# Attention heads of a four-layer kernel: queries and keys as two 12-bit parts in fp32r words instead of three bf16 parts

## The reference, cut to what matters

```python
# layer 0, one sequence of 2048
scores = einsum('bhtd,bhsd->bhts', q, k) * scale       # scale = 8 ** -0.5
attn = softmax(scores, axis=-1)
out = einsum('bhts,bhsd->bhtd', attn, v)

# layer 3: q and k turned by rope, and causal
score = einsum('bhqd,bhkd->bhqk', rope(Q), rope(K)) / sqrt(8)
score = score - 1e10 * (1 - tril)
weights = softmax(score - max(score), axis=-1)
attn = einsum('bhqk,bhkd->bhqd', weights, V)
```

## Time and profile before

| what | value |
|---|---|
| time, median of 3 runs (lowest, highest) | 1925.89 us (1922.76, 1926.48) |
| span of the profiled execution, first to last instruction | 1923.2 us |
| own time of the profiled execution | not recorded apart from its span |
| PE matmul busy | 1697.7 us (88%) |
| DVE busy | 1435.9 us (75%) |
| ACT busy | 1143.8 us (59%) |
| POOL busy | 307.7 us (16%) |
| heads of layer 0 | from 47.3 to 744.9 us |
| heads of layer 3 | from 1396.4 to 1850 us |

### The profile page before, as it was taken

How to read it: one execution, slowest core, us unless ns; L and a number is a source line. 1 busy time by engine, 2 the same in 40 slices (tenths; PEclk the granted TensorE clock), 3 DMA queues, 4 the chain that set the end, 5 groups by cost and what they waited for, 6 DMA issues and landing times. The chain is left out here.

```text
span 1923.2 us, 44062 instructions
## 1 busy us (share of the span) xinstructions
PE 1697.7 (88%) x17529; PEld 802.7 (42%) x17529; DVE 1435.9 (75%) x2718; ACT 1143.8 (59%) x2262; POOL 307.7 (16%) x460
## 2 busy tenths in 40 slices
PE   3799999999999995889997798892779999999977
PEld 2222222222222222434444544781425555555556
DVE  5889999999999954665555507656779999999735
ACT  3268888888888894332222244452317777777754
POOL 0103000010000100000000345443012232210123
PEclk8789999999999998799997899996759999999988
DMA  4112111121111012033233269861511111111132
GB/s 143 36 30 81 63 55 51 55 81 64 55 51 34 28 28 59 33 66 106 95 89 144 69 225 333 268 186 48 191 33 30 33 37 37 34 36 36 28 76 70
DMA packets 78037, 154.52 MB, mean 80 GB/s; under 512 B 18684, under 2 KB 35964, under 8 KB 74136
## 3 DMA queue, kind: packets, MB, share of 16 engines
q1 hardware_dynamic: 63034, 121.38, 20.0%
q0 software_dynamic: 14384, 29.29, 4.9%
q10 hardware_dynamic: 414, 1.04, 0.2%
HBM read 102.23 MB, written 48.89 MB: 79 GB/s over the span
## 5 line engine op out<-in xcount | busy, mean ns | idle before, releaser
L856 ACT ACTIVATE heads_probs<-heads_pS 128x512 f32<-128x512 f32 (+3 forms) x1664 | 851.6, 573 | 187.9 <-PE heads_pS L725 172.2
L881 DVE TENSOR_REDUCE heads_run_max<-heads_pM 128x1 f32<-128x1024 f32 x512 | 592.6, 1216 | 54.6 <-PE heads_pM L747 53.3
L787 PE MATMUL heads_pO<-heads_probs,heads_vh 128*32 128x512 f32 (+2 forms) x3328 | 438.1, 570 | 3.2 <-ACT heads_probs L856 1.4
L725 PE MATMUL heads_pS<-heads_qs,heads_ks 75*32 75x512 bf16 (+3 forms) x4160 | 392.7, 370 | 3.8 <-ACT heads_probs L856 1.6
L892 DVE TENSOR_REDUCE heads_run_max<-heads_pM 128x1 f32<-128x512 f32 x384 | 246.7, 684 | 17.2 <-PE heads_pM L725 13.7
L725 PE MATMUL heads_pS<-heads_q_first,heads_ks 75*32 75x512 bf16 x2496 | 234.4, 377 | 7.9 <-ACT heads_probs L856 7.4
L725 PEld LDWEIGHTS heads_pS<-heads_qs,heads_ks 75*32 75x32 bf16 x4160 | 117.3, 95 | 171.2 <-issue 81.3
L725 PE MATMUL heads_pM<-heads_ks,heads_qs 72*32 72x512 bf16 (+3 forms) x1600 | 174.6, 359 | 1.1 <-DVE heads_run_max L892 0.5
L889 DVE CUSTOM_DVE_ANT_0 heads_masked_out<-heads_pM,heads_mask_end 128x128 bf16<-128x128 f32 (+3 forms) x256 | 120.7, 485 | 19.5 <-PE heads_pM L725 17.2
L787 PEld LDWEIGHTS heads_pO<-heads_probs,heads_vh 128*32 128x32 f32 x3328 | 106.7, 110 | 53.3 <-issue 7.1
L725 PEld LDWEIGHTS heads_pS<-heads_q_first,heads_ks 75*32 75x32 bf16 x2496 | 71.3, 95 | 122.4 <-ACT heads_probs L856 66.8
(11 more groups left out here) (388 smaller groups left out, 2369.0 us busy)
## 6 DMA issues: line engine op xcount, KB each, us to landing
top_weights<-k_comb_dram SPq DMA_DIRECT2D x128, 128.0 KB, 3.0
second_w<-in_L_W_dram SPq DMA_DIRECT2D x12, 1024.0 KB, 10.8
k_hid_slots_dram<-k_zeros SPq DMA_DIRECT2D x8, 1152.0 KB, 5.0
k_h_slots_dram<-second_work SPq DMA_DIRECT2D x48, 192.0 KB, 3.1
second_work<-k_hid_slots_dram SPq DMA_DIRECT2D x48, 192.0 KB, 4.3
k_parts_dram<-proj_part SPq DMA_DIRECT2D x12, 512.0 KB, 4.1
heads_ks<-k_parts_dram SPq DMA_DIRECT2D x63, 96.0 KB
heads_qs<-k_parts_dram SPq DMA_DIRECT2D x40, 96.0 KB
```

The lines of the kernel that those rows point to most:

```text
L725: mm = pe.matmul(out[cols, :], still[:, cols], moving, start=start, stop=stop)
L787: mm = pe.matmul(pO[k * 32:k * 32 + VW, int(second), o:BLK], vh[c][:, t, :], probs[u % 2][:, k * BLK + o:(k + 1) * BLK], start=first_chunk ...
L856: act.activation(probs[u % 2][:, k * BLK + c0 - b * BLK:(k + 1) * BLK], pS[:, slot, 0:c1 - c0], ACT.Exp)\
L881: dve.reduce_max(run_max[:, i, blocks[0][0] // 2:blocks[0][0] // 2 + 1], both.rearrange("p k c -> p (k c)"), AX.X).then_inc(taken, 2)
```

## The change

Queries and keys are split into two parts instead of three: the high part is the float32 word with its low 12 bits cleared (an integer AND on DVE), the low part the exact rest. Both are kept as 4-byte words of type fp32r. Four products of 8 dimensions give 32 rows. The stack is loaded twice, on partitions 0 to 31 and 64 to 95; rows 32 (and 96) are zero against one, rows 33 to 35 (and 97 to 99) hold the three parts of the maxima. Each fill block and each chunk is one matmul on 64 of the 128 rows, and `turns` alternates the halves from one matmul to the next. `by_columns` goes. The diagonal of layer 3 is added in two matmuls of 64 rows, with swapped copies of the mask for the other half of the contraction. The max rows go out in six transfers instead of three, the stacks in 6 instead of 14 (layer 0) or 8 (layer 3). The presets are four memsets for each stack pair, in 4-byte words. In layer 0 the fills of every unit, not of every second one, are placed after chunk 1 and chunk 3.

```diff
+ROUNDED = mybir.dt.float32r
-STK = PARTS * PARTS * HD
+SPLIT = 2
+HIGH_BITS = -4096
+STK = SPLIT * SPLIT * HD
+HALF = 64
+MAX_ROW = STK + 1
...
+            for to, at in ((slice(0, HALF), slice(HALF, P)), (slice(HALF, P), slice(0, HALF))):
+                dve.tensor_copy(K.ident_swapped[to, :], K.ident[at, :]).then_inc(made, 1)
+                dve.tensor_scalar(K.neg_below_swapped[to, :], masks[at, 1, :], NEG, None, ALU.mult).then_inc(made, 1)
...
-                if n < N:
-                    act.wait_ge(whole, n + 1)
-                    act.activation(parts[w][0][:, cols], full[:, n % 4, :], ACT.Copy).then_inc(hi, 1)
                 if n >= 1:
                     w, b = divmod(n - 1, NB)
-                    act.wait_ge(r1, n)
-                    act.activation(parts[w][1][:, b * BLK:(b + 1) * BLK], rest[:, (n - 1) % 4, :], ACT.Copy)\
-                       .then_inc(mid, 1)
+                    act.wait_ge(masked, n)
+                    act.activation(parts[w][0][:, b * BLK:(b + 1) * BLK], rest[:, (n - 1) % 4, :], ACT.Copy)\
+                       .then_inc(hi, 1)
...
-                    dve.tensor_tensor(rest[:, n % 4, :], full[:, n % 4, :], parts[w][0][:, b * BLK:(b + 1) * BLK],
-                                      ALU.subtract).then_inc(r1, 1)
+                    dve.tensor_scalar(rest[:, n % 4, :].bitcast(I32), full[:, n % 4, :].bitcast(I32), HIGH_BITS, None,
+                                      ALU.bitwise_and).then_inc(masked, 1)
...
+def query_parts(K, h):
+    return K.parts[0][h].rearrange("a d t -> (a d) t").unsqueeze(0).broadcast_to([SPLIT, SPLIT * HD, T])
+def key_part(K, h, r):
+    return K.parts[1][h, r].unsqueeze(0).broadcast_to([SPLIT, HD, T])
...
+            h = ROUND * p + c
+            for half in (0, HALF):
+                yield qs[c % ROUND][half:half + STK, :].bitcast(F32), query_parts(K, h), stacked[c % ROUND]
+                for r in range(SPLIT):
+                    rows = slice(half + r * SPLIT * HD, half + (r + 1) * SPLIT * HD)
+                    yield ks[c % ROUND][rows, :].bitcast(F32), key_part(K, h, r), stacked[c % ROUND]
...
+        def set_spare_rows(engine, i):
+            for n, (stack, half) in enumerate(itertools.product((qs[i], ks[i]), (0, HALF))):
+                rows = slice(half + HALF // 2, half + HALF)
+                engine.memset(stack[rows, :].bitcast(F32), float(n // 2)).then_inc(rows_set[i], 1)
+                engine.wait_ge(rows_set[i], n + 1)
...
-                for a in range(PARTS):
-                    sp.dma_start(qs[c % ROUND][STK + a:STK + a + 1, :].rearrange("o (t c) -> o t c", c=P),
-                                 max_rows[a * NT:(a + 1) * NT, :]).then_inc(rows_in, 16)
+                for row in (MAX_ROW, HALF + MAX_ROW):
+                    for a in range(PARTS):
+                        sp.dma_start(qs[c % ROUND][row + a:row + a + 1, :].bitcast(F32).rearrange("o (t c) -> o t c", c=P),
+                                     max_rows[a * NT:(a + 1) * NT, :].bitcast(F32)).then_inc(rows_in, 16)
...
+                for k, (b, w) in enumerate(blocks):
+                    at = next(turns)
+                    rows = slice(at, at + STK + 1)
+                    mm = pe.matmul(pM[:, bank_of(c, j, k), 0:w], qs[c % ROUND][rows, i * P:(i + 1) * P],
+                                   ks[c % ROUND][rows, b * BLK:b * BLK + w], start=True, stop=True)
...
-                mm = by_columns(pS[:, slot, 0:c1 - c0], ks[c % ROUND][0:STK + PARTS, u * P:(u + 1) * P],
-                                qs[c % ROUND][0:STK + PARTS, c0:c1], True, not diag)
+                at = next(turns)
+                rows, mask = slice(at, at + MAX_ROW + PARTS), slice(at, at + HALF)
+                mm = pe.matmul(pS[:, slot, 0:c1 - c0], ks[c % ROUND][rows, u * P:(u + 1) * P],
+                               qs[c % ROUND][rows, c0:c1], start=True, stop=not diag)
                 if diag:
-                    mm = by_columns(pS[:, slot, 0:P], K.ident_b[:, :], K.neg_below[:, :], False, True)
+                    pe.matmul(pS[:, slot, 0:P], K.ident_b[mask, :], K.neg_below[mask, :], start=False, stop=False)
+                    mm = pe.matmul(pS[:, slot, 0:P], K.ident_swapped[mask, :], K.neg_below_swapped[mask, :], start=False,
+                                   stop=True)
...
-                        behind = [(len(new) // 2, 1 + 2 * i)[u % 2] for i in range(len(todo))]
+                        behind = [1 + 2 * i for i in range(len(todo))]
...
-            dve.memset(ks[0][64:96, :], 1.0).then_inc(ones_set[0], 1)
+            set_spare_rows(dve, 0)
```

More of the change, by code:

```diff
@@ L7 @@
+import itertools
 from contextlib import ExitStack
@@ L297, in head_projections @@
         rest = S.sb("rest", [P, 4, BLK])
-        parts = [[S.sb(f"part{w}{a}", [P, T], BF16) for a in range(PARTS)] for w in range(2)]
+        parts = [[S.sb(f"part{w}{a}", [P, T], ROUNDED) for a in range(SPLIT)] for w in range(2)]
         pq = S.ps("pq", [P, 4, BLK])
@@ L333, in _ @@
             for w in range(2):
-                for a, done in enumerate((hi, mid, lo)):
+                for a, done in enumerate((hi, lo)):
                     sp.wait_ge(done, NB * (w + 1))
-                    sp.dma_start(K.parts[w][:, a, :, :], parts[w][a][:, :]).then_inc(stored[w], 16)
+                    sp.dma_start(K.parts[w][:, a, :, :], parts[w][a][:, :].bitcast(F32)).then_inc(stored[w], 16)
                     if rope and (w, a) == (1, 0):
@@ L462, in _ @@
                     dve.tensor_tensor(dst, src, bv.unsqueeze(1).broadcast_to([P, TPB, D]), ALU.add).then_inc(vkept, 1)
[L465 to L467 removed]
+def query_parts(K, h):
+    return K.parts[0][h].rearrange("a d t -> (a d) t").unsqueeze(0).broadcast_to([SPLIT, SPLIT * HD, T])
+def key_part(K, h, r):
+    return K.parts[1][h, r].unsqueeze(0).broadcast_to([SPLIT, HD, T])
 def first_queries(K, causal):
[L472 to L477 removed]
+    for half in (0, HALF):
+        yield K.first_q[half:half + STK, :].bitcast(F32), query_parts(K, 0)
 def causal_plan(causal):
@@ L581, in load_stacks @@
         def load_stacks(p, c):
-            h, at = ROUND * p + c, 0
-            for r, n0, n1 in PRODUCTS:
-                n = n1 - n0
-                q = K.parts[0][h, n0:n1].rearrange("a d t -> d a t")
-                k = K.parts[1][h, r].unsqueeze(1).broadcast_to([HD, n, T])
-                for first in (0,) if causal or at >= HALF else (0, HALF):
-                    rows = slice(first + at, first + at + n * HD)
-                    for full, half, src in ((qs, qd, q), (ks, kd, k)):
-                        yield (half if first else full)[c % ROUND][rows, :], src, stacked[c % ROUND]
-                at += n * HD
-        def load_first_keys(queue, turn):
-            keys = list(load_stacks(0, 0))[1::2]
-            for i in range(turn, len(keys), 2):
-                dst, src, sem = keys[i]
-                if i == len(keys) - 1:
-                    queue.wait_ge(ones_set[0], 1)
-                queue.dma_start(dst, src).then_inc(sem, 16)
+            h = ROUND * p + c
+            for half in (0, HALF):
+                yield qs[c % ROUND][half:half + STK, :].bitcast(F32), query_parts(K, h), stacked[c % ROUND]
+                for r in range(SPLIT):
+                    rows = slice(half + r * SPLIT * HD, half + (r + 1) * SPLIT * HD)
+                    yield ks[c % ROUND][rows, :].bitcast(F32), key_part(K, h, r), stacked[c % ROUND]
+        def load_first_keys(queue, turn):
+            keys = [load for n, load in enumerate(load_stacks(0, 0)) if n % (1 + SPLIT)]
+            for dst, src, sem in keys[turn::2]:
+                queue.dma_start(dst, src).then_inc(sem, 16)
+        def set_spare_rows(engine, i):
[3 more added lines that the diff above has]
+                engine.wait_ge(rows_set[i], n + 1)
         def split_max(queue, g):
@@ L720, in _ @@
         def _(pe):
-            def by_columns(out, still, moving, start, stop):
-                for g in range(P // VW):
-                    cols = slice(g * VW, (g + 1) * VW)
-                    mm = pe.matmul(out[cols, :], still[:, cols], moving, start=start, stop=stop)
-                return mm
+            turns = itertools.cycle((0, HALF))
             def bank_of(c, j, k):
@@ L2477, in recurrent_layers @@
         K.slot_i, K.place_i = sb("slot_i", [P, 2, NT], I32), sb("place_i", [P, 2, NT], I32)
-        K.parts = [dram(f"parts{w}", (HEADS, PARTS, HD, T), BF16) for w in range(2)]
+        K.parts = [dram(f"parts{w}", (HEADS, SPLIT, HD, T)) for w in range(2)]
         K.head_out = dram("head_out", (HEADS, HD + 1, T))
```

78 lines of the change are left out of this document (27 added, 51 removed).

## The result

The changed kernel takes 2644.9 us (median of 4 runs, 2644.3 to 2646.0); the kernel before took 1926.18 us beside it. The ratio is 1.374, with a 95% interval of 1.372 to 1.376. The prediction was 1873, in a range of 1850 to 1926.

The account below looks back on a forecast made before the run. PE was taken to bound both heads stages, less strictly in layer 3; -34.5 - 22.5 + 1 + 2 - 4 + 4.5 + 0.5 = -53 us on 1923.2 gave 1870, 1873 for the median, range 1850 to 1926.

Parts of the forecast that it names:

- the full clock: Both heads stages: PE priced at full clock, a pass of 512 columns at 0.215 us, a layer 0 unit at 2.34.
- a rival at 0.06: Heads stages: PE streams less, so the clock falls to 1.2 GHz, 3.8 us a layer 0 unit for 2.34; chance 0.06.
- a clock below 1.00 in the steady heads: Heads stages: a granted clock under 1.00 was named as one sign that the forecast is wrong.
- The price of the matmul: Fills and chunks on PE: a pair of new matmuls on two halves takes one pass, 0.215 us.
- rivals of two and of four passes: New matmuls on PE: two passes or no side-by-side halves, near 2027 us, chance 0.09; four passes, near 2660, chance 0.03.
- counted as hidden: New matmuls on PE: weight loads hide under matmuls; otherwise a pair costs 0.28 us for 0.215, a layer 0 unit 2.2.
- DVE's floor: Layer 0 heads: DVE needs 36.6 us a head; 0.9 left for waits makes 37.5, gain 34.5 us (0 to 48).
- the rival on the order on PE: Heads stages: chunks waiting for ACT and fills for DVE alternate, heads stay near 39.5 and 25.6, 1915 to 1932; chance 0.12.
- Stacks: nothing: Stack loads in both layers: spread under a head of 24 us or more at DMA share 0.13 to 0.18, cost nothing.
- Presets: Memsets at stage starts: layer 3's first fill 4.5 us later, 8 to 9 after the stage starts; layer 0 costs 0.
- Max rows: Six max row transfers in the heads: the reserve of 1.8 us is used up, adding 2 us in all (0 to 15).
- Projection of layer 0: Layer 0 projection: blocks at about 1.25 us for 1.76, 4 us earlier (2 to 6), bigger stores taking little.

Follow-up runs that it names:

- the run with earlier loads: Changed kernel with fills of 61 and chunks of 64 rows, head dimension outermost in stack transfers, these sent every second chunk: 2017.09 us (kernel before there: 1928.15).
- the bf16 halves: Changed kernel's halves with three bf16 parts, six products, rows 61/64, projections as before the change, transfers every second chunk: 1925.54 us (kernel before there: 1928.15).
- dense matmuls: Changed kernel with twelve float32 matmuls of 512 columns on PE before the first chunk of each heads stage: 2727.6 us (kernel before there: 2003.6).

## Why the prediction was wrong

**The step that failed: "the full clock" carried over.** Every term of the sum was priced at 2.4 GHz. The clock was a rival at 0.06, and it was weighed by the wrong thing: how long PE streams. What it held against the rival, that the last head of layer 0 streams 79% of the time, with pauses, at 1.00, is true of chunks that use 75 rows in four column groups. The changed kernel streams without a pause and has 0.50. What the runs showed in its place: fp32r matmuls on 33 and 36 rows, two side by side, ran at 0.50 in all steady heads, 4.06 us a unit where 2.34 was forecast: the prediction's own sign of being wrong, "a clock below 1.00 in the steady heads". At that clock the rival's own figure, 3.8 us a unit, was near the 4.06; what lies above it stands at the ends of a unit (first pair to second 0.59 us for 0.42, last chunk to sum 0.72). Its size can be read from the run with earlier loads, which does the same work at the full clock: layer 0 takes 728.3 us there and layer 3 490.7, so by that comparison 370 of the 408.6 us and 232 of the 275.2 are the clock. The Trainium skill (TensorE: Matmul & The Clock Gate, What's actually happening) says that the low clock is the state of an idle engine and that activity lifts it. The trace differs: 600 and 900 us of 100% busy stay at 0.50 here.

**The price of the matmul held.** One pass, two halves side by side: the rivals of two and of four passes are out. Their times were less wrong than the forecast, for another reason.

**Weights "counted as hidden": wrong.** The prediction's own alternative, a pair of 0.28 and a unit of 2.2 on PE, was closer, and still too low: 0.35 from the first pair to the second and 2.61 us a unit. So at the full clock, which the run with earlier loads has, layer 0 is at 42.1 us a head for the 37.5 forecast, and layer 3 at 28.3 for 24.3. Even with the clock right, the answer was slower, by 89 us.

**DVE's floor held, what lies above it did not.** 36.6 us a head was DVE's pace, and four reductions in 4.61 us in the same stage bear it out. The 0.9 us left for engines that wait for each other was too little: the bf16 halves, at the full clock and with light weights, give 39.0 us a head, 2.4 above the floor, not 37.5. The forecast gain of 34.5 us in layer 0 would have been 12. So what the rival on the order on PE describes, waits of the two engines for each other, would have taken some two thirds of layer 0's gain, by the reading above.

**"Stacks: nothing": wrong.** They were priced by bytes and by the share of the DMA engines in the steady stretch. The first keys of each stage have no cover, and they came over two engines: 14.6 us later in layer 0, 9.6 in layer 3, and ahead of layer 3's stage another 13.4 while the first queries' loads, over two engines too, ran beside the last store. That store was also issued 2.1 us late, behind them on SP. In layer 3 the loads became a wait in each head as soon as PE was fast.

**Presets: nearly right.** With the keys out of the way, layer 3's first fill comes 9.7 us after the stage's start, where 8 to 9 were forecast, and waits for DVE. **Max rows: nearly right.** In the run with earlier loads PE waits for them in four heads of layer 3, 4.4 us in all and 2.9 of it in one head, where 2 us were put in the sum; in the changed kernel it never waits for them in layer 3's steady heads. **Projection of layer 0: half right.** ACT's last activation ends 5.1 us earlier (33.4 for 38.5), but the stage, which waits for four stores of 1 MB instead of six of 0.5 MB, ends only 0.5 us earlier (46.9 for 47.3); "bigger stores take little" took all but that.

What stays open: why bf16 words with 33 and 36 rows get the full clock in most heads of layer 0 and fp32r words with these rows never; why 65 to 69 rows alone got it in layer 3 and not in layer 0; and how much of the longer fp32r unit is the load of weights and how much the switch between shapes.

## What to carry to other kernels

A busy PE isn't a PE at full clock: before packing matmuls into fewer rows, compare the rows at work at a time with those of a stretch whose granted clock is known, and read the clock first in the profile after. Zero rows in the contraction cost no time that these runs show, and they gave 23 us a head of layer 0 back. Price a transfer by how many engines its outermost dimension lets it use, and ask of each one that was hidden who waits for it in the first head, where nothing hides it. Take an engine's floor from the distance of its starts, and leave room above it where two engines fill and empty the same two buffers.

## What the runs showed of the hardware

- PE busy for 899 of 900 us at 1.2 GHz, with 33 + 36 rows in use; 28 more rows in the chunks, of zero times one, and the same stream has 2.4 GHz.
- With 33 and 36 rows the granted clock went from 1.00 to 0.50 by 140 us, where dense matmuls had ended at 137.5, though PE was busy but for 0.45 us.
- The same matmuls on one half instead of two alternating ones: 1.2 GHz instead of 2.4, and 87.3 us a head of layer 0 for 42.0.
- fp32r: one column a cycle (0.42 us for 512 at 1.2 GHz), and 185 ns for 64x128 weights at 2.4 GHz where bf16 has 94.
- A transfer with an outermost dimension of 2 moved over two of 16 DMA engines, at 53 GB/s, where transfers with 8 there moved 98 to 175.
